# Context of tile 0 loaded ahead of the positions; VectorE's work of the first steps, a bank and the turned maxima of tile 3 ordered anew

## The chip, the core and the metric

The kernel runs on one core of one Trainium2 chip. A core has TensorE (PE, matrix products, which go to PSUM), VectorE (DVE), ScalarE (ACT), GpSimd (POOL), and SyncE (SP), which here only issues DMAs. Every engine works through its own instructions in order and waits on semaphores for the others. The metric is the device time of one execution in microseconds (us); lower is better.

## What is computed

One transformer block on 1024 tokens of 512 features, in fp32: cross attention with rotary positions and 32 heads that share 8 key and value heads, then a mixture of low-rank experts. In batches of 64 tokens each query sees the 64 context rows of its own batch.

```python
def block(x, c, pos):
    h = layernorm(x)
    q, k, v = h @ Wq, c @ Wk, c @ Wv
    q, k = q*cos + rotate_half(q)*sin, k*cos + rotate_half(k)*sin
    p = softmax(q @ k.T / sqrt(16))          # 32 heads of 16, 8 of k and v
    x = x + (p @ v) @ Wo
    h = layernorm(x)
    scores = (h @ Wr.T) @ keys.T             # 64 experts, the best 16 of them
    gate = softmax over the best 16, 0 elsewhere
    z = (h @ A.T) * gate for each group of 8 columns
    return x + (z @ B.T) * 2
```

## The kernel before

The tokens are 8 tiles of 128. Large products are done with operands split into a high and a low part (hi, lo): ScalarE rounds the high part, VectorE or GpSimd subtracts to get the low part, and TensorE adds three products (hi by hi, hi by lo, lo by hi). Tile 0 and the keys and values of tile 1 are done raw, in full fp32, since their weights are not split yet.

The order of every engine is written out by hand in five stages: `first()`, `second()`, `step(i)` for i = 1 and 2, `late_step(i)` for i = 3 to 5, and `last()`. In step i the attention of tile i is finished, the scores of tile n = i + 1 are made, q, k and v of tile p = i + 2 are projected, and, from i = 2 on, the experts of tile f = i - 2 are done. Step 1 has no tile f; it does work that comes once instead. Engines meet through counting semaphores, and several PSUM banks (ps_t0, ps_t1, ps_w0, ps_w1, ps_s) have many users one after another.

What the change touches:
- The head. ScalarE's queue issues the positions (`pos_sb`, L609) and the context of tile 0 (`cT_in`, L610). SyncE's queue issues x of tile 0, then the weights. VectorE copies the positions (L1174) ahead of aggregating the statistics of tile 0; from these GpSimd makes 1/std (L412) and VectorE xh (L1191), the normalised x, which TensorE turns (L1359).
- `attend(t, meanwhile)` on VectorE: a transpose of the sums of values (o_s, L1052), reciprocals (L1057), a product (o_t, L1061), a transpose back (o_n, L1067). `meanwhile` is work between the first transpose and the reciprocals. `q_low(t)` is the low part of the turned q (qT_lo, L1009).
- `top(t, b)` takes maxima of the scores, `m_parts(t)` splits them (m_split, L1044 and L1046), TensorE turns them (`turn_m`, L1458), and ScalarE copies them out: `m_out`, one copy of mT (L695) up to tile 2, two large copies into q_stack (L691) from tile 3 on. Then come the turned scores (L1483; L1470 for the stacked tiles 3 to 6), ScalarE's exponentials (L702) and the values (L1500).
- From tile 4 on, q is projected from the raw x (`DIRECT = 4`), and its mean is taken out with the negated column sums of Wq. `wq_sum` adds them, `sum_columns` (L1401) spreads them with TensorE into the bank `SUMS`, and `sums_out` copies them (L645). `statistics1(t)` (L943 to L952) and GpSimd's `deviation1(t)` (L412, then cs_q) give mean and 1/std of tile t.
- `residual(t)` adds x (L1075) and makes the mean x_mean (L1080), which ScalarE's centred x (x_c, L717) needs; `x2_low` is L1095. In step 2 `route(0)` is the choice of experts, whose last instruction makes gate (L1127). `split_lo` on GpSimd makes the low parts of weights, b_lo among them (L403).
- `up_high(f)` on TensorE is the high part of the experts' last product, eight matmuls in chunks k = 0 to 3.

Two rules of the code on banks matter: `qT_bank(3)` is ps_t0, and so is `kT_bank(3)`; `x2T_bank(0)` and `x2T_bank(1)` are ps_t1.

Of the kernel before, what the change touches and what calls it, by code (L numbers as in the profile page):

```python
# [21 lines left out]
FIRST = 3  # L22
STACKED = (3, 4, 5, 6)
QUADS = (4, 5, 6, 7)
DIRECT = 4
# [32 lines left out]
def build(nc, x, xT, cT, pos, wq, wqT, wkv, wo, aT, router, bT, out):  # L58
    ctx = ExitStack()
    with ctx:  # L60
# [130 lines left out]
        def x2_of(t):  # L191
            return (x2[:, 0, :], x2[:, 1, :], wq_sb[:, 0, :])[t % 3]

        SUMS = ps_t1[:]

        def wqT_of(k):
            return (xT_raw[:].rearrange("p k q -> p (k q)"), res[:], z_sb, zg)[k]
# [20 lines left out]
        def qT_bank(t):  # L218
            return ps_t1 if t > LATE else ps_t0
# [180 lines left out]
        def _(pool):  # L400
            def split_lo(lo, raw, hi, high, low, k):
                pool.wait_ge(high, k + 1)
                pool.tensor_tensor(lo[:, k, :], raw[:, k, :], hi[:, k, :].bitcast(F32),  # L403
                                   ALU.subtract).then_inc(low, 1)

            def deviation1(t):
                pool.wait_ge(stat1, 3 * t + 3)
                if t >= 1:
                    pool.wait_ge(xh_ok, min(t, DIRECT))
                if t > DIRECT:  # L410
                    pool.wait_ge(cs_q_ok, t - DIRECT)
                pool.tensor_tensor(rstd1[:], ve1[:], neg_half[:], ALU.pow).then_inc(rstd1_ok, 1)  # L412
                if t >= DIRECT:
                    pool.wait_ge(rstd1_ok, t + 1)
                    pool.wait_ge(q_rot, 2 * t)
                    pool.tensor_scalar(cs_q[:], cs[:, t, :], rstd1[:], None, ALU.mult).then_inc(cs_q_ok, 1)
                elif t >= 1:
                    pool.wait_ge(rstd1_ok, t + 1)
                    pool.tensor_scalar(shift1[:], mv1[:, 0:1], rstd1[:], -1.0, ALU.mult, ALU.mult)\
                        .then_inc(shift1_ok, 1)  # L420
# [125 lines left out]

            def step(i):
                f, n, p = i - 2, i + 1, i + 2
                if p >= DIRECT:
                    deviation1(p)  # L550
                if f >= 0:
                    gated(f)
                else:
                    split_lo(b_lo, b_sb, b_hi, b_h, b_l, 0)
                deviation2(i - 1)
                o_low(i)
                k_blocks(p, 0)
                k_blocks(p, 1)
                if f < 0:
                    x_low(p + 1)  # L560
                rotated_q(p)
                if f >= 0:
                    x_low(p + 1)
                c_low(p + 1)
                if f < 0:
                    for k in range(1, DK):
                        split_lo(b_lo, b_sb, b_hi, b_h, b_l, k)
# [38 lines left out]

        @block.scalar
        def _(act):
            act.dma_start(pos_sb[:], pos).then_inc(ld_pos, 16)  # L609
            act.dma_start(cT_in[:, 0], cT[0]).then_inc(ld_c[0], 16)  # L610

            def split_hi(hi, raw, high, k):
                act.activation(hi[:, k, :], raw[:, k, :], ACT.Copy).then_inc(high, 1)
# [321 lines left out]
        def _(dve):  # L935
# [45 lines left out]
            def k_low(t):  # L981
                dve.wait_ge(kT_hi_ok, t + 1)
                if t >= 1:
                    dve.wait_ge(k_bd_ok, 2 * t)
                dve.tensor_tensor(kT_lo[:], kT_bank(t), kT_hi[:].bitcast(F32), ALU.subtract)\
                   .then_inc(kT_lo_ok, 1)
# [250 lines left out]

            def second():
                rotate_k(2)
                q_low(1)  # L1240
                attend(0)
                top(1, 0)
                top(1, 1)
                m_parts(1)
                k_low(2)
                rotate_q(2)
                x_low(3)
                residual(0)
                statistics2(0)

            def step(i):
                f, g, n, p = i - 2, i - 1, i + 1, i + 2
                if p >= DIRECT:
                    statistics1(p)
                if f >= 0:
                    route(f)
                    x2_low(g)
                attend(i, lambda: q_low(n))
                rotate_k(p)
                top(n, 0)  # L1260
                if f >= 0:
                    rotate_q(p)
                top(n, 1)
                k_low(p)
                if f < 0:
                    m_parts(n)
                    x2_low(g)
                    rotate_q(p)
                else:
                    m_parts(n)  # L1270
                    z_low(f)
                residual(i)
                statistics2(i)
                if f >= 0:
                    result(f)
# [60 lines left out]
        def _(pe):  # L1336
# [77 lines left out]
            def turn_q(t):  # L1414
                pe.wait_ge(q_r_ok, t + 1)
                pe.wait_ge(kT_lo_ok, t + 1)
                turn(qT_bank(t), q_r, REP).then_inc(qT_ps, 1)

            def quad_scores(t):
# [101 lines left out]

            def turn_x2(t):
                pe.wait_ge(x2_c_ok, t + 1)
                if t == 1:
                    pe.wait_ge(sums_ok, 1)
                turn(x2T_bank(t), x2_c, DK).then_inc(x2T_ps, 1)

            def down_high(t, half, chunks=range(DK)):
# [99 lines left out]
            def step(i):  # L1628
                f, g, n, p = i - 2, i - 1, i + 1, i + 2
                turned_scores(i)  # L1630
                if f >= 0:
                    pe.wait_ge(x2_ok, i)
                    project_down(f, 0)
                    if f >= 1:
                        pe.wait_ge(res_ok, f)
                    else:
                        pe.wait_ge(q_rot, 2 * p)
                    project_q(p, [0, 1])
                    pe.wait_ge(z_ok, 2 * f + 1)
                    project_down(f, 1)  # L1640
                    turn_x2(g)
                else:
                    pe.wait_ge(q_rot, 2 * p)
                    project_q(p, [0, 1, 2])
                values(i)
                turn_q(n)
                if f < 0:
                    turn_x2(g)
                if f >= 0:
                    pe.wait_ge(z_ok, 2 * f + 2)  # L1650
                else:
                    pe.wait_ge(x2_ok, i)
                project_kv(p)
                if f >= 0:
                    project_q(p, [2])
                scores(n, 0)
                scores(n, 1)
                if f >= 0:
                    pe.wait_ge(x2T_lo_ok, i)
                    turn_zg(f)  # L1660
                    turn_k(p)
                project_q(p, [3]).then_inc(q_ps, 1)
                if f < 0:
                    turn_k(p)
                pe.wait_ge(v_st_ok, p + 1)
                project_out(i)
                if f >= 0:
                    pe.wait_ge(q_rot, 2 * p + 2)
                    up_high(f)
                turn_m(n)  # L1670
                if f >= 0:
                    up_low(f)
                    turn_q(p)
                else:
                    pe.wait_ge(x2T_lo_ok, i)
                    sum_columns()

            def late_step(i):
# [152 lines left out]
```

## Time and profile before

| | before |
|---|---|
| median of 3 runs | 167.12 us (166.97 to 168.05) |
| the profiled execution | 167.25 us, span 165.5 us |
| PE busy | 159.5 us, 96% of the span |
| DVE busy | 135.7 us, 82% |
| ACT busy | 95.3 us, 58% |
| POOL busy | 89.5 us, 54% |
| chain that ended last, by engine | PE 78%, DVE 12%, issue 4%, DMA 3%, ACT 2% |
| TensorE's granted clock | 1.00 of full speed |

The span runs from the first to the last instruction of the profiled execution. The chain is followed back from the last instruction, at each step to what released it. TensorE is busy nearly throughout; it stands still in the first 6 us and at a few waits.

### The profile page before, as it was taken

The numbers are of one execution on the slowest core, as the hardware profiler recorded it, in microseconds if no ns is written. First come the engines' busy times: TensorE is split into PE (matmuls) and PEld (weight loads), VectorE is DVE, ScalarE is ACT, GpSimd is POOL, SyncE is SP. The second block draws the span as 40 slices with busy tenths as digits, with TensorE's granted clock in tenths as the row PEclk, the third lists the DMA queues.
The fourth block names the chain that finished last, engine by engine and source line by source line (L and its number), as shares of the span: only waits on it lengthen the run. The fifth ranks groups of instructions, "written<-read, shape, count | busy, mean of one in ns | idle before, by whom it ended". The sixth has DMA issues, their size and how long they took to land.

```text
span 165.5 us, 4197 instructions
## 1 busy us (share of the span) xinstructions
PE 159.5 (96%) x1437; PEld 128.8 (78%) x1437; DVE 135.7 (82%) x394; ACT 95.3 (58%) x215; POOL 89.5 (54%) x115
## 2 busy tenths in 40 slices
PE   7799999999999999999999999999999999999993
PEld 2556786777878887879888888979789886789883
DVE  1969886995998899799888998799886999868562
ACT  3588999899657443942579147842479065414210
POOL 6479999999889843724942099015360304220300
DMA  4999962303315234426452453114410000000013
GB/s 142 380 411 388 408 200 67 133 4 122 99 32 160 50 92 99 119 54 181 101 125 54 114 151 87 47 46 145 101 52 31 4 0 29 36 2 4 0 63 127
DMA packets 12116, 18.45 MB, mean 111 GB/s; under 512 B 2496, under 2 KB 5056, under 8 KB 11840
## 3 DMA queue, kind: packets, MB, share of 16 engines
q1 hardware_dynamic: 11808, 17.93, 34.9%
q10 hardware_dynamic: 288, 0.27, 0.5%
q8 instruction: 11, 0.18, 0.5%
q14 instruction: 9, 0.07, 0.1%
HBM read 11.11 MB, written 2.10 MB: 80 GB/s over the span
## 4 chain that ended last, share of the span: by engine, by line
PE 78%; DVE 12%; issue 4%; DMA 3%; ACT 2%; ACTq 0%; DVEq 0%
PE ps_w L1346 12%; PE ps_w L1347 11%; PE ps_w L1351 10%; PE ps_t L1359 6%; PE ps_s L1430 4%; PE ps_w L1339 3%; PE ps_w L1341 3%; PE ps_w L1340 3%; DVE ps_s L1034 3%; DMA cT_in<-cT 3%; PE ps_t L1500 3%; PE ps_s L1470 2%; PE ps_w L1563 2%; PE ps_w L1569 2%; PE ps_t L1351 2%
## 5 line engine op out<-in xcount | busy, mean ns | idle before, releaser
L481 POOL TENSOR_TENSOR late<-late,gate 128x512 f32<-128x512 f32 x7 | 7.6, 1081 | 32.6 <-DVE gate L1127 17.6
L702 ACT ACTIVATE eT<-ps_s 128x512 f32<-128x512 f32 x32 | 17.0, 602 | 1.8 <-PE ps_s L1489 1.0
L466 POOL TENSOR_TENSOR oT_lo<-o_n,oT_hi 128x512 fp32r<-128x512 f32 x8 | 10.4, 1295 | 9.0 <-ACT oT_hi L710 9.0
L1346 PE MATMUL ps_w<-am_hi,x2T_hi 128*128 128x288 f32 x44 | 12.7, 311 | 0.0
L1347 PE MATMUL ps_w<-am_lo,x2T_hi 128*128 128x288 f32 x44 | 12.0, 296 | 0.0
L1346 PE MATMUL ps_w<-b_hi,zT_hi 128*128 128x512 f32 (+1 forms) x28 | 11.0, 399 | 0.0
L412 POOL TENSOR_TENSOR rstd<-ve,neg_half 128x1 f32<-128x1 f32 x8 | 4.4, 554 | 12.2 <-DVE ve L952 10.8
L1024 DVE TENSOR_REDUCE ps_s<-ps_s 128x8 f32<-128x512 f32 x16 | 10.6, 688 | 0.3 <-PE ps_s L1430 0.2
L1034 DVE TENSOR_REDUCE ps_s<-ps_s 128x8 f32<-128x512 f32 x16 | 10.4, 691 | 0.5 <-PE ps_s L1449 0.3
L1339 PE MATMUL ps_w<-wq_hi,xT_hi 128*128 128x512 f32 x26 | 10.7, 413 | 0.0
L754 ACT ACTIVATE zT_hi<-ps_t 128x512 fp32r<-128x512 f32 x7 | 4.2, 598 | 11.2 <-PE ps_t L1359 11.2
L1347 PE MATMUL ps_w<-b_lo,zT_hi 128*128 128x512 f32 (+1 forms) x28 | 10.5, 379 | 0.0
L1341 PE MATMUL ps_w<-wq_hi,xT_lo 128*128 128x512 f32 x26 | 10.3, 395 | 0.0
L1340 PE MATMUL ps_w<-wq_lo,xT_hi 128*128 128x512 f32 x26 | 10.3, 394 | 0.0
L691 ACT ACTIVATE q_stack<-ps_s 32x1024 fp32r<-32x1024 f32 x8 | 7.7, 1010 | 4.2 <-PE ps_s L1458 4.2
L740 ACT ACTIVATE late<-ps_w 128x288 f32<-128x288 f32 x5 | 2.1, 412 | 13.1 <-PE ps_w L1351 13.0
L1346 PEld LDWEIGHTS ps_w<-am_hi,x2T_hi 128*128 128x128 f32 x44 | 8.3, 189 | 1.1 <-ACT late L736 0.4
L437 POOL TENSOR_TENSOR q_r<-q_a,q_b 128x512 f32<-128x512 f32 x7 | 9.1, 1295 | 0.0
L663 ACT ACTIVATE v_bd<-v_st 64x64 f32<-64x64 f32 x32 | 8.1, 252 | 0.6
L1347 PEld LDWEIGHTS ps_w<-am_lo,x2T_hi 128*128 128x128 f32 x44 | 8.3, 189 | 0.0
L426 POOL TENSOR_TENSOR cT_lo<-cT_in,cT_hi 128x512 fp32r<-128x512 f32 x6 | 7.8, 1294 | 0.0
L1009 DVE TENSOR_TENSOR qT_lo<-ps_t,qT_hi 128x512 fp32r<-128x512 f32 x8 | 5.4, 680 | 2.8 <-ACT qT_hi L679 2.8
(283 smaller groups left out, 554.0 us busy)
## 6 DMA issues: line engine op xcount, KB each, us to landing
x_sb<-x SPq DMA_DIRECT2D x8, 256.0 KB, 7.0
q_stack<-qT_hi SPq DMA_DIRECT2D x32, 64.0 KB, 2.0
cT_in<-cT SPq DMA_DIRECT2D x7, 256.0 KB, 3.8
out<-res SPq DMA_DIRECT2D x7, 256.0 KB, 2.0
wq_sb<-wq SPq DMA_DIRECT2D x4, 256.0 KB, 5.2
late<-wo SPq DMA_DIRECT2D x1, 1024.0 KB, 7.9
am_sb<-aT SPq DMA_DIRECT2D x1, 1024.0 KB, 9.3
b_sb<-bT SPq DMA_DIRECT2D x1, 1024.0 KB, 7.8
```

The source lines that it names most:

```text
L437: pool.tensor_tensor(q_r[:].rearrange("p (r k d) -> p k r d", r=REP, k=KVH), q_a[:].rearrange("p (k r d) -> p k r d", r=REP, k=KVH), q_b[: ...
L466: pool.tensor_tensor(oT_lo[:], o_n[:].rearrange("p (b r q) -> p r b q", b=2, r=REP), oT_hi[:].bitcast(F32), ALU.subtract).then_inc(oT_lo_o ...
L702: act.activation(eT[:, c].rearrange("p b n -> p (b n)"), ps_s[:, c, :], ACT.Exp)\
L1024: dve.tensor_reduce(neg_top[:, b, :, rp].rearrange("p (c h) -> p c h", h=2), ps_s[:, :, at:at + P].rearrange("p c (h k) -> p c h k", h=2), ...
L1034: dve.tensor_reduce(neg_top[:, b, HALF_H * half:HALF_H * (half + 1), :], ps_s[:, 2 * (1 - b) + half, :].rearrange("p (r h k) -> p h r k", ...
L1339: pe.matmul(dst, hi(k), w_hi[:, k, cols], start=(k == 0), stop=False)
L1340: pe.matmul(dst, hi(k), w_lo[:, k, cols], start=False, stop=False)
L1341: mm = pe.matmul(dst, lo(k), w_hi[:, k, cols], start=False, stop=(k == DK - 1))
L1346: pe.matmul(dst, hi(k), w_hi[:, k, cols], start=(k == 0), stop=False)
L1347: pe.matmul(dst, hi(k), w_lo[:, k, cols], start=False, stop=False)
L1351: mm = pe.matmul(dst, lo(k), w_hi[:, k, cols], start=False, stop=(k == DK - 1))
L1359: mm = pe.transpose(dst[:, P * k:P * (k + 1)], src[:, P * k:P * (k + 1)], ident[:])
```

## The change

It has five edits in the order of work, and one of a bank.

ScalarE issues the context of tile 0 ahead of the positions. The rows of ScalarE's queue at its start, before (-) and after (+), where pos_sb holds the positions and cT_in the context:

```order
-L609 DMA pos_sb<-pos 128x8
-L610 DMA cT_in<-cT 128x512
+L609 DMA cT_in<-cT 128x512
+L610 DMA pos_sb<-pos 128x8
 L766 ACT_TABLE_LOAD
```

The two loads change places; nothing else moves on ScalarE.

On VectorE, in `second()`, around `attend(0)`: L1009 is `q_low(1)`, L1052 the transpose of the values of tile 0, L1057 the reciprocals.

```order
-L1009 TENSOR_TENSOR qT_lo<-ps_t,qT_hi 128x4x2x64
 L1052 STREAM_TRANSPOSE o_s<-ps_s 128x1024
+L1009 TENSOR_TENSOR qT_lo<-ps_t,qT_hi 128x4x2x64
 L1057 RECIPROCAL ps_s<-o_s 128x16 x2
 L1061 TENSOR_TENSOR o_t<-o_s,ps_s 128x16x16 x2
```

`q_low(1)` has moved behind the transpose. The statistics of tile 4 (L943, L950, L952) have moved from the start of step 2 to the end of `second()`, and GpSimd's `deviation1(4)` with them, to the start of step 1.

On VectorE in step 1, behind the maxima of tile 2 (L1034): L985 is kT_lo of tile 3, L1044 and L1046 split the maxima, L1075 and L1080 are the residual of tile 1 and its mean, L1095 is x2T_lo of tile 0.

```order
 L1034 TENSOR_REDUCE ps_s<-ps_s 128x8 x4
-L985 TENSOR_TENSOR kT_lo<-ps_t,kT_hi 128x128
-L1044 CAST m_split<-ps_s 128x8x16
-L1046 TENSOR_TENSOR m_split<-ps_s,m_split 128x8x16
+L1044 CAST m_split<-ps_s 128x8x16
+L1046 TENSOR_TENSOR m_split<-ps_s,m_split 128x8x16
+L985 TENSOR_TENSOR kT_lo<-ps_t,kT_hi 128x128
+L1075 SCALAR_TENSOR_TENSOR late,x_sum<-ps_w,x_sb 128x512
+L1080 TENSOR_SCALAR x_mean<-x_sum 128x1
 L1095 TENSOR_TENSOR x2T_lo<-ps_t,x2T_hi 128x512
```

The maxima are split before kT_lo, and the residual and its mean stand ahead of x2T_lo and of rotating q, where they had been behind both.

The column sums go to the bank ps_t0. There they wait for kT_lo of tile 3, not for x2T_lo of tile 0, and it is the turning of q of tile 3 that waits until they are copied out, not the turning of x of tile 1.

On TensorE in step 2 the turned maxima of tile 3 come ahead of the last chunk of `up_high(0)`, 0.5 us of matmuls earlier in the order.

```diff
-        SUMS = ps_t1[:]
+        SUMS = ps_t0[:]
...
                 if t >= DIRECT:
                     pool.wait_ge(rstd1_ok, t + 1)
-                    pool.wait_ge(q_rot, 2 * t)
+                    if t > DIRECT:
+                        pool.wait_ge(q_rot, 2 * t)
...
             def second():
                 rotate_k(2)
-                q_low(1)
-                attend(0)
+                attend(0, lambda: q_low(1))
...
                 statistics2(0)
+                statistics1(4)
...
             def turn_q(t):
                 pe.wait_ge(q_r_ok, t + 1)
                 pe.wait_ge(kT_lo_ok, t + 1)
+                if t == FIRST:
+                    pe.wait_ge(sums_ok, 1)
                 turn(qT_bank(t), q_r, REP).then_inc(qT_ps, 1)
...
             def turn_x2(t):
                 pe.wait_ge(x2_c_ok, t + 1)
-                if t == 1:
-                    pe.wait_ge(sums_ok, 1)
...
                 if f >= 0:
                     pe.wait_ge(q_rot, 2 * p + 2)
-                    up_high(f)
+                    up_high(f, [0, 1, 2])
                 turn_m(n)
                 if f >= 0:
+                    up_high(f, [3])
                     up_low(f)
                     turn_q(p)
                 else:
-                    pe.wait_ge(x2T_lo_ok, i)
+                    pe.wait_ge(kT_lo_ok, p + 1)
                     sum_columns()
```

## Rows read from the trace of the kernel before

**Rows 1.** The chain that ended last: start us, us, what.

```profile
1.22 4.38 DMA cT_in<-cT
...
47.24 0.65 PE ps_t L1401 x4
```

**Rows 2.** Timeline, 4 to 7 us: start, us, engine line op out<-in xcount [idle<-releaser].

```profile
4.23 0.15 DVE L1174 CAST pos_f<-pos_sb 128x8 f32<-128x8 int32 x1
...
5.51 0.54 DVE L1191 TENSOR_SCALAR xh<-x_sb,mv,rstd 128x512 f32<-128x512 f32 x1
...
6.67 0.60 PE L1359 MATMUL ps_t<-ident,xh 128*128 128x128 f32 x4
```

**Rows 3.** DMAs issued before 2 us (last column us to landing), traffic 2.5 to 3.0.

```profile
x_sb<-x SPq DMA_DIRECT2D x1, 256.0 KB, 2.8
cT_in<-cT ACTq DMA_DIRECT2D x1, 256.0 KB, 4.4
pos_sb<-pos ACTq DMA_DIRECT2D x1, 4.0 KB, 3.0
...
DMA packets 173, 0.17 MB, mean 337 GB/s; under 512 B 92, under 2 KB 92, under 8 KB 173
```

**Rows 4.** Timeline, 25 to 29 us: values, transpose and reciprocals of tile 0.

```profile
25.67 1.09 PE L1500 MATMUL ps_s<-eT,v_bd 64*32 64x256 f32 x32
...
27.02 1.24 DVE L1052 STREAM_TRANSPOSE o_s<-ps_s 128x1024 f32<-128x1024 f32 x1
...
28.30 0.37 DVE L1057 RECIPROCAL ps_s<-o_s 128x16 f32<-128x16 f32 x2
```

**Rows 5.** Timeline, 37 to 41 us: the same of tile 1.

```profile
37.79 1.09 PE L1500 MATMUL ps_s<-eT,v_bd 64*32 64x256 f32 x32
...
38.99 1.25 DVE L1052 STREAM_TRANSPOSE o_s<-ps_s 128x1024 f32<-128x1024 f32 x1 [1.83 <-PE ps_s L1500]
...
40.75 0.36 DVE L1057 RECIPROCAL ps_s<-o_s 128x16 f32<-128x16 f32 x2
```

**Rows 6.** Timeline, 45 to 48 us, end of step 1.

```profile
45.79 0.28 DVE L985 TENSOR_TENSOR kT_lo<-ps_t,kT_hi 128x128 fp32r<-128x128 f32 x1
45.98 0.28 DVE L1044 CAST m_split<-ps_s 128x128 fp32r<-128x128 f32 x1
...
47.12 0.38 ACT L695 ACTIVATE mT<-ps_s 128x256 fp32r<-128x256 f32 x1 [0.77 <-PE ps_s L1458]
...
47.82 0.39 PE L1483 MATMUL ps_s<-qT_hi,k_bd_hi 32*128 32x256 f32 x4
```

**Rows 7.** Timeline, 49 to 55 us, start of step 2.

```profile
49.21 0.72 ACT L717 ACTIVATE x_c<-late,x_mean 128x512 f32<-128x512 f32 x1 [0.68 <-DVE x_mean L1080]
...
50.10 0.68 DVE L943 BATCH_NORM_STATS2 bn<-x_sb 128x6 f32<-128x512 f32 x1
...
51.27 0.24 ACT L733 ACTIVATE s_sb<-ps_w 128x64 f32<-128x64 f32 x1
...
52.29 0.19 PEld L1346 LDWEIGHTS ps_w<-am_hi,x2T_hi 128*128 128x128 f32 x1 [0.42 <-ACT late L736]
...
54.71 0.56 POOL L412 TENSOR_TENSOR rstd<-ve,neg_half 128x1 f32<-128x1 f32 x1
```

**Rows 8.** Timeline, 65 to 69 us: the maxima of tile 3.

```profile
65.14 0.29 DVE L1046 TENSOR_TENSOR m_split<-ps_s,m_split 128x128 fp32r<-128x128 f32 x1
...
65.83 0.38 PE L1458 MATMUL ps_s<-ident,m_split 128*128 128x128 f32 x2
...
66.25 1.93 ACT L691 ACTIVATE q_stack<-ps_s 32x1024 fp32r<-32x1024 f32 x2 [2.82 <-PE ps_s L1458]
...
68.23 0.86 PE L1470 MATMUL ps_s<-q_stack,k_stack 128*128 128x256 f32 x5 [0.16 <-ACT q_stack L691]
```

**Rows 9.** Timeline, 50 to 55 us, then line L1127 in all: ns min/median/max.

```profile
50.96 3.80 POOL L403 TENSOR_TENSOR b_lo<-b_sb,b_hi 128x512 fp32r<-128x512 f32 x3
...
54.09 0.72 DVE L1127 TENSOR_SCALAR gate<-e_top,g_scale 128x64 f32<-128x64 f32 x1
...
L1127 DVE TENSOR_SCALAR gate<-e_top,g_scale x8: 254/255/724, 54.1 to 157.2; 128x64 f32<-128x64 f32 x8
```

More of the change, by code:

```diff
@@ L548, in step @@
                 f, n, p = i - 2, i + 1, i + 2
-                if p >= DIRECT:
-                    deviation1(p)
                 if f >= 0:
@@ L553, in step @@
                 else:
+                    deviation1(p + 1)
                     split_lo(b_lo, b_sb, b_hi, b_h, b_l, 0)
@@ L608, in _ @@
         def _(act):
+            act.dma_start(cT_in[:, 0], cT[0]).then_inc(ld_c[0], 16)
             act.dma_start(pos_sb[:], pos).then_inc(ld_pos, 16)
-            act.dma_start(cT_in[:, 0], cT[0]).then_inc(ld_c[0], 16)
             def split_hi(hi, raw, high, k):
@@ L1249, in second @@
                 statistics2(0)
+                statistics1(4)
             def step(i):
                 f, g, n, p = i - 2, i - 1, i + 1, i + 2
-                if p >= DIRECT:
-                    statistics1(p)
                 if f >= 0:
@@ L1263, in step @@
                 top(n, 1)
-                k_low(p)
                 if f < 0:
                     m_parts(n)
+                    k_low(p)
+                    residual(i)
                     x2_low(g)
@@ L1269, in step @@
                 else:
+                    k_low(p)
                     m_parts(n)
                     z_low(f)
-                residual(i)
+                    residual(i)
                 statistics2(i)
```

## The prediction

> **What bounds the kernel now.** I read the chain that ended last first. From 48 us to 128 us it is nearly all TensorE, piece after piece, so a delay or a gain that reaches TensorE before 68 us is carried to the end as it is. What matters is where, before that, the chain is not TensorE's own work. There are five such places, and each edit of this change touches one of them.
> The head: the chain starts with the load of the context of tile 0 (1.22 us, 4.38 long), and TensorE's first raw product follows at once [rows 1]. The second link is the first turned tile of x: VectorE copies the positions at 4.23, aggregates the statistics behind that copy, and writes xh from 5.51 to 6.05; TensorE turns it at 6.67 [rows 2]. So xh has some 0.6 us to spare and the context has none.
> `second()`: the values of tile 0 (25.67), the transpose (27.02), the reciprocals (28.30) [rows 4]. The chain passes over VectorE here.
> Step 1: the chain is VectorE's from 38.99 until the column sums, which TensorE starts at 47.24 once `x2_low(0)` is done [rows 1, 6].
> Step 2, two places: a weight load that waits for ScalarE's copy of z [rows 7], and the two big ScalarE copies of the turned maxima of tile 3, for which TensorE stands until 68.23 [rows 8].
>
> **The change part by part.**
> *1. Context ahead of positions.* The ScalarE queue now issues the context at 0.78 instead of 1.22 and the positions behind it. Landing took 4.4 us for the context, 3.0 for the positions and 2.8 for x of tile 0, which SyncE issued at the same moment [rows 3]. The context's data now runs beside those of x. From 2.5 to 3.0 us all queues together moved 337 GB/s [rows 3]; the context's 262 KB at that rate take 0.78 us, by which x can land later if the two share evenly (0 if x goes first). The positions' small packets no longer share x's time, so I take 0.70 rather than 0.78. The positions come last either way, but the bytes ahead of them are the same, so their landing is about that of the later of the two and adds nothing to it. The copy of the positions then moves from 4.23 to about 4.93, and xh ends at 6.75 instead of 6.05 [rows 2]. The context is there by then, so TensorE's first raw products are out of the way, and the turning starts at about 6.83 against 6.67: **+0.16**. Bounds: below, x and the positions not delayed at all, the turning starts 0.4 earlier, by the 0.44 that the issue moves less what TensorE needs after xh; above, the positions land only after a context that still takes 4.4 us, at 5.2, so the copy is 0.97 late, xh ends at 7.02, and the turning starts at 7.10: +0.43.
> The Trainium skill (DMA: Bandwidth & Descriptors, section Queues, rings and completion order) has the descriptors of one queue consumed in ring order on each DMA engine, and the engine taking turns between queues. No row of before shows a small transfer behind a large one on the ScalarE queue. By that rule the upper bound is a real possibility and not a mishap; it is the second rival below.
> *2. `q_low(1)` after the transpose of tile 0.* Before, it ran in VectorE's idle time ahead of the transpose. In step 1 the same pair already stands in the new order, so I read its cost there: values at 37.79, transpose 1.20 later, `q_low` behind it, reciprocals 1.76 after the transpose's start [rows 5]. Put on tile 0: values at 25.67, transpose 26.87, reciprocals 28.63, against 28.30 [rows 4]. The transpose starts 0.15 earlier and the reciprocals come 0.33 later: **+0.33**. All that follows on VectorE (the context of tile 0, the maxima of tile 1) and through ScalarE the output projection is on the chain. Bounds: -0.15, if the subtraction were free, and +0.58, the whole 0.69 less what starts early.
> *3. Statistics of tile 4 ahead of step 1.* Three VectorE instructions, one of 0.68 [rows 7] and two small ones, about 1.0 us together, move to where VectorE sat idle 1.83 us before the transpose of tile 1 [rows 5]; part 2 moves both ends of that gap, so they fit: 0. If the cover were gone they would cost 1.0. In step 2 they stood ahead of routing, which waited for s_sb anyway: 0 as well. GpSimd's pair (the power, 0.56 [rows 7], and cs_q, less than that) moves ahead of the first b_lo, where its later `o_low(1)` had idle time that part 2 only widens.
> *4. Column sums in the other bank, maxima of tile 2 first.* With the new order, m_split's cast starts where kT_lo started, 45.79, 0.19 before its old place [rows 6]; with the 0.33 of part 2 it is 0.14 later than before, and TensorE, whose output projection also slid 0.33, finds it ready. The sums now wait for kT_lo, which follows the two instructions of m_split (0.29 for one [rows 8]) and ends about 46.9, before TensorE has turned the maxima; the wait for x2T_lo is gone. What is late next is ScalarE's mT: it started at 47.12, now at 47.45, ends 0.37 later, and the turned scores start at about 47.86 against 47.82 [rows 6]. So of the 0.33 that came in, 0.04 goes out: **-0.29**. Bounds: 0, and -0.41 should mT not slide. Queued behind the moved kT_lo are GpSimd's k_bd_lo, x_low(4), c_low(4) and b_lo; rotating q of tile 3 falls behind the residual, so that b_lo starts about 1.35 late, but none is needed by TensorE for another 1 us or more.
> *5. Residual of tile 1 earlier.* ScalarE's x_c waited 0.68 for x_mean at 49.21, and its exponentials and s_sb (51.27) stood behind it [rows 7]. x_mean is now done before 48. At 52.29 a weight load had waited 0.42 for ScalarE's late (z) [rows 7], so that one load of 0.19 was exposed: **-0.15**. Bounds 0 and -0.26.
> *6. Maxima of tile 3 turned before the last chunk of `up_high(0)`.* m_split is ready at 65.14 + 0.29 = 65.43; TensorE turned it at 65.83, ScalarE began to copy at 66.25, and TensorE stood for the second copy until 68.23 [rows 8]. Now the turning starts at about 65.47. TensorE's other work is the same, plus an exposed weight load. 65.83 - 65.47 is 0.36, less a little for that load: **-0.33**. Bounds 0 (something else holds the stacked scores) and -0.41.
> Sum: 0.16 + 0.33 - 0.29 - 0.15 - 0.33 = -0.28 us. Span 165.5 becomes 165.2, and that execution, 167.25 with 1.75 around the span, 166.97. The median of the runs is 0.13 below it: 167.12 - 0.28 = **166.84, I say 166.85 us**.
>
> **The rivals.**
> *Slower: the gate of tile 0 misses its turn (0.10).* VectorE's gate took 0.72 at 54.09 and ended where a b_lo of GpSimd ended; its median over all tiles is 0.255 [rows 9]. GpSimd ran three b_lo from 50.96 in 3.80 us, 1.27 each [rows 9]. These now start about 1.35 later and end at 53.6, 54.8 and 56.1. A gate that starts near its old 54.09 is let go at 54.8 and x2T_lo is not late. If it starts after 54.8 it is held until 56.1, which is some 0.85 more than x2T_lo can bear; all of VectorE's step 2 up to m_split follows. Sum +0.57: 167.7. It decides from some 0.7 of delay in routing. Against it: routing starts earlier if part 5 holds.
> The Trainium skill (SBUF — State Buffer, on the shared pair of ports) calls this an exclusive lock held for a whole instruction; the trace agrees, 0.72 against 0.255.
> *No change: positions behind the context (0.20).* The upper bound of part 1, +0.43 in place of +0.16: sum -0.01, 167.1. It is what the ring order of the skill would make at its worst. For it: the context took 4.4 us, against 2.8 for x. Against it: the context then had the first weights beside it.
> *Faster: the head gains (0.17).* x is not slowed, and the positions land in time: -0.4 in place of +0.16: sum -0.84, 166.3. For it: the transfers of the first 3 us don't fill the engines at once. Against it: the rate from 2.5 us on.
> *Part 6 does nothing (0.08).* The stacked scores would stand on their DMAs, not on ScalarE's copy: sum +0.05, 167.2. Against it: the row at 68.23 names ScalarE [rows 8].
>
> **How the numbers follow.** Forecast 0.45, the rivals 0.10, 0.20, 0.17 and 0.08. The forecast alone gives 166.6 to 167.1 (parts 2 and 4 each to 0.2). Rivals reach from 166.3 to 167.7; leaving out a tenth on each side, the range is 166.2 to 167.6. A measurement of this kernel can tell about 1% (1.7 us) from no change. None of the cases reaches it. Only several bounds together would (-1.6 if all parts went well, +1.0 if all went badly), so faster by over 1% has 0.05, slower 0.03, within 1% 0.92.
>
> **What would show it.** Part 1: the copy of the positions at 4.9 (5.2 and later is the second rival, 4.3 the third), the first turning at 6.8. Part 2: reciprocals of tile 0 some 1.76 after the transpose's start. Part 4: column sums directly behind the turned maxima, the turned scores within 0.1 of where they would be without part 2's loss. Part 5: no wait of ScalarE's x_c for x_mean. Part 6: TensorE's wait for q_stack, 0.4 now, gone. The slower rival: a gate that ends after 55. The forecast would be wrong as a whole if TensorE were not continuous from 68 to 128 us and the gains were given back there, in waits for the stacked tiles' DMAs.

## The result

| | before | after |
|---|---|---|
| median of 20 runs each | 167.51 us (166.75 to 168.05) | 168.31 us (167.49 to 169.05) |
| ratio | | 1.0051, 95% interval 1.0038 to 1.0064 |
| the profiled execution | 167.25 us, span 165.5 us | 167.49 us, span 165.8 us |
| DVE busy | 135.7 us | 136.6 us |
| ACT busy | 95.3 us | 95.6 us |
| TensorE's granted clock | 1.00 | 1.00 |

The change makes the kernel slower by 0.5%, 0.85 us. The forecast was 0.28 us faster, 166.85 us, and its range ended at 167.6. The difference is within 1%, to which the forecast gave 0.92, but it is a loss where a gain was forecast. The profiled execution of the kernel after is the fastest of its 20, so its span is only 0.3 us above that of before: the traces below show where the time moves, the medians how much.

The first and the fourth part of the page of the kernel after: busy time of the engines, and shares of the span in the chain that ended last.

```profile
PE 159.3 (96%) x1437; PEld 128.6 (78%) x1437; DVE 136.6 (82%) x394; ACT 95.6 (58%) x215; POOL 89.6 (54%) x115
...
PE 52%; POOL 21%; SPq 9%; issue 7%; DVE 6%; DMA 4%; ACT 0%; ACTq 0%; POOLq 0%; DVEq 0%
```

The work is the same, but the chain is not. Before, 78% of it was TensorE's and SyncE's queue was not in it at all. Now it runs over GpSimd and then over SPq, SyncE's issuing of DMAs. The chain itself, kernel after, 48 to 69 us (start us, us, what):

```profile
48.55 1.31 POOL xT_lo L433
49.87 0.33 SPq L293
...
50.25 0.66 SPq L328
50.95 0.60 SPq L328
...
54.78 1.76 SPq L328
56.58 0.60 SPq L328
...
59.20 0.56 SPq L340
...
65.50 0.59 SPq L340
66.13 1.98 DMA q_stack<-qT_lo
68.16 1.22 PE ps_s L1472 x8
```

L293 is `load_xT(5)`, which may overwrite xT_raw only when GpSimd has made xT_lo from it. Queued behind it on SyncE are the copies that stack keys (L328) and turned queries (L340) of tile 3: 24 DMAs, 0.64 us from one issue to the next. The last is issued at 66.13 (before: 65.06) and lands 1.98 us later, and TensorE's stacked scores stand on it. Of the 1.07 by which it is later, 0.38 is there at the first stacked copy (49.87 to 50.25); the rest is nearly all one issue, the row at 54.78, of 1.76 us, where the longest before took 1.05. That part is mostly the draw of this one execution: in the 20 traces of this case the longest issue at this place takes 0.92 to 1.76 us, and this trace has the longest. What the change does to the queue is the 0.38; that it costs time in the medians too is shown by the experiments below and not by this trace.

### The profile page after: what moved, and what is told of

Its sections match the earlier page's. It is cut to its first block, busy times and chain, and to the rows that moved or that the text cites. A ratio compares the mean times of both kernels' runs of the same rounds, so it can differ in the third digit from the quotient of the medians.

```text
span 165.8 us, 4196 instructions
## 1 busy us (share of the span) xinstructions
PE 159.3 (96%) x1437; PEld 128.6 (78%) x1437; DVE 136.6 (82%) x394; ACT 95.6 (58%) x215; POOL 89.6 (54%) x115
## 4 chain that ended last, share of the span: by engine, by line
PE 52%; POOL 21%; SPq 9%; issue 7%; DVE 6%; DMA 4%; ACT 0%; ACTq 0%; POOLq 0%; DVEq 0%
PE ps_w L1346 8%; PE ps_w L1347 7%; PE ps_w L1351 7%; SPq L328 5%; PE ps_t L1359 4%; SPq L340 4%; PE ps_s L1432 4%; POOL am_lo L403 3%; POOL wo_lo L403 3%; POOL wq_lo L403 3%; PE ps_t L1502 3%; PE ps_s L1472 2%; POOL k_bd_hi L458 2%; DMA pos_sb<-pos 2%; PE ps_t L1346 2%
## 5 line engine op out<-in xcount | busy, mean ns | idle before, releaser
L1034 DVE TENSOR_REDUCE ps_s<-ps_s 128x8 f32<-128x512 f32 x16 | 10.4, 692 | 0.5 <-PE ps_s L1451 0.3
L1351 PE MATMUL ps_w<-am_hi,x2T_lo 128*128 128x288 f32 x44 | 7.6, 295 | 0.0
```

What stands on the lines that cost most here:

```text
L1034: dve.tensor_reduce(neg_top[:, b, HALF_H * half:HALF_H * (half + 1), :], ps_s[:, 2 * (1 - b) + half, :].rearrange("p (r h k) -> p h r k", ...
L1351: mm = pe.matmul(dst, lo(k), w_hi[:, k, cols], start=False, stop=(k == DK - 1))
```

## Where the parts moved things

The head. Landing of the first DMAs after issue (last column us), then the timeline, kernel after (start, us, engine, line, what, [idle before <- releaser]).

```profile
cT_in<-cT ACTq DMA_DIRECT2D x1, 256.0 KB, 3.5
x_sb<-x SPq DMA_DIRECT2D x1, 256.0 KB, 3.3
pos_sb<-pos ACTq DMA_DIRECT2D x1, 4.0 KB, 3.9
```

```profile
4.14 0.69 DVE L1172 BATCH_NORM_STATS2 bn<-x_sb 128x6 f32<-128x512 f32 x1 [2.95 <-DMA x_sb<-x]
...
5.06 1.10 PE L1563 MATMUL ps_w<-wkv_sb,cT_in 128*128 128x256 f32 x4 [0.17 <-issue]
...
5.17 0.17 DVE L1174 CAST pos_f<-pos_sb 128x8 f32<-128x8 int32 x1 [0.34 <-DMA pos_sb<-pos]
...
6.41 0.54 DVE L1191 TENSOR_SCALAR xh<-x_sb,mv,rstd 128x512 f32<-128x512 f32 x1
...
7.01 0.44 PE L1359 MATMUL ps_t<-ident,xh 128*128 128x128 f32 x2 [0.85 <-DVE xh L1191]
```

The context lands at 4.3 instead of 5.6 (0.79 + 3.5 against 1.22 + 4.4 [rows 3]) and TensorE's raw product starts 0.67 earlier. x lands later too: VectorE starts its statistics at 4.14 instead of 3.62, so 0.52 is lost there. The positions land at 5.15 instead of 3.8, VectorE stands at their copy for 0.34, xh comes 0.90 later in all, and TensorE then stands 0.85 for it: the first turned tile starts at 7.01 instead of 6.67 [rows 2].
The Trainium skill (DMA: Bandwidth & Descriptors, section Queues, rings and completion order) has descriptors of one queue consumed in ring order on each DMA engine. The traces agree: behind 256 KB the 4 KB of positions took 3.9 us, ahead of them 3.0, and they landed 0.9 us after the context.

`second()`. The same view, 26 to 30 us.

```profile
26.08 1.09 PE L1502 MATMUL ps_s<-eT,v_bd 64*32 64x256 f32 x32
...
27.28 1.25 DVE L1052 STREAM_TRANSPOSE o_s<-ps_s 128x1024 f32<-128x1024 f32 x1 [2.11 <-PE ps_s L1502]
...
28.46 0.65 DVE L1009 TENSOR_TENSOR qT_lo<-ps_t,qT_hi 128x512 fp32r<-128x512 f32 x1
...
29.03 0.36 DVE L1057 RECIPROCAL ps_s<-o_s 128x16 f32<-128x16 f32 x2
```

From the values to the reciprocals 2.95 us, against 2.63 [rows 4]; from the transpose to them 1.75, where the forecast read 1.76 off tile 1 [rows 5].

End of step 1 and start of step 2.

```profile
47.19 0.28 DVE L985 TENSOR_TENSOR kT_lo<-ps_t,kT_hi 128x128 fp32r<-128x128 f32 x1
...
47.55 1.04 POOL L458 TENSOR_TENSOR k_bd_lo<-kT_lo,half_mask 128x512 fp32r<-128x512 f32 x1 [0.87 <-DVE kT_lo L985]
...
47.82 0.38 ACT L695 ACTIVATE mT<-ps_s 128x256 fp32r<-128x256 f32 x1 [0.73 <-PE ps_s L1460]
...
48.25 0.39 PE L1485 MATMUL ps_s<-qT_hi,k_bd_hi 32*128 32x256 f32 x4
```

```profile
48.33 0.15 DVE L1080 TENSOR_SCALAR x_mean<-x_sum 128x1 f32<-128x1 f32 x1
48.55 1.30 POOL L433 TENSOR_TENSOR xT_lo<-xT_raw,xT_hi 128x512 fp32r<-128x512 f32 x1
...
48.88 0.72 ACT L717 ACTIVATE x_c<-late,x_mean 128x512 f32<-128x512 f32 x1
```

The reciprocals came in 0.73 late (28.30 to 29.03); the turned scores are 0.43 late (47.82 to 48.25), the values' transpose of tile 2 only 0.12 (55.86 to 55.98), so parts 4 and 5 gave back 0.30 and 0.31. But kT_lo is 1.40 late (45.79 [rows 6] to 47.19), and with it GpSimd's k_bd_lo, and xT_lo of tile 4, which ends at 49.85.

The maxima of tile 3.

```profile
65.25 0.29 DVE L1046 TENSOR_TENSOR m_split<-ps_s,m_split 128x128 fp32r<-128x128 f32 x1
...
65.59 0.44 PE L1460 MATMUL ps_s<-ident,m_split 128*128 128x128 f32 x2
...
66.07 1.93 ACT L691 ACTIVATE q_stack<-ps_s 32x1024 fp32r<-32x1024 f32 x2 [2.54 <-PE ps_s L1460]
...
68.16 1.10 PE L1472 MATMUL ps_s<-q_stack,k_stack 128*128 128x256 f32 x7 [0.28 <-DMA q_stack<-qT_lo]
```

m_split is 0.11 late, the turning 0.24 early, ScalarE's first copy 0.18 early (66.25 [rows 8] to 66.07). All eight stacked scores then run in a row from 68.16 (the eighth starts past this view's end), behind a wait for a DMA. Before, three of them ran from 67.47 on, and five from 68.23 [rows 8]. They end at 69.38 against 69.09: the 0.18 won has become 0.29 lost, and tile 7's values still carry 0.25 (139.56 to 139.81).

## The experiments

All are compared with the kernel before, measured beside it on the same chip. A ratio of 0.001 is 0.17 us. The 1.0051 of the whole change was measured apart from them, and the difference of two such ratios is uncertain by 0.4 to 0.6 us where nothing else is said. Line numbers shift by a few between kernels.

**The change less one part: head.** The kernel after with the positions first again.

```diff
-            act.dma_start(cT_in[:, 0], cT[0]).then_inc(ld_c[0], 16)
             act.dma_start(pos_sb[:], pos).then_inc(ld_pos, 16)
+            act.dma_start(cT_in[:, 0], cT[0]).then_inc(ld_c[0], 16)
```

> The changed kernel with the positions again ahead of the context on ScalarE's queue. Theory A (two early losses, the head and q_low of tile 1, that reach the end through SyncE's queue: they make x_low(4) late, which holds the load of xT of tile 5 and behind it the 24 DMAs of the stacked tile 3): the positions' copy back at 4.2, everything up to step 1 about 0.4 earlier, and since SyncE is then less late, 0.3 to 0.6 of the 0.85 given back: ratio to before 1.001 to 1.003. Theory B (the head is the whole loss, q_low and SyncE's queue cost nothing): ratio 0.998 to 1.000. Theory C (the head costs 0.35 to 0.4 in the first stage, but TensorE has made it up by the end, and the loss is elsewhere): ratio stays 1.004 to 1.006.

Measured 0.9992 [0.9969, 1.0016]. In the changed kernel the head costs 0.99 us (1.0051 less 0.9992; 0.5 to 1.4 by the two intervals). The ratio lies in theory B's range, but B also says that q_low and SyncE's queue cost nothing, and the runs below speak against that.

**Less q_low.** The kernel after with `q_low(1)` ahead of `attend(0)` again.

```diff
-                attend(0, lambda: q_low(1))
+                q_low(1)
+                attend(0)
```

> The changed kernel with q_low of tile 1 again ahead of the transpose of tile 0. Theory A: the reciprocals of tile 0 come 0.33 sooner behind the same head, 0.2 to 0.4 of the time is given back: ratio to before 1.002 to 1.004. Theory B: no difference from the changed kernel, 1.005. Theory C: 1.004 to 1.006.

Measured 1.0007 [0.9983, 1.003]: in the changed kernel it costs 0.74 us (0.3 to 1.2), more than the 0.2 to 0.4 that theory A expected.

**Less both**, which leaves parts 3 to 6.

> The changed kernel with both early edits undone; what is left are the edits of step 1, of step 2 and of the bank. Theory A: the stacked scores of tile 3 start no later than before, and the turned maxima 0.3 to 0.5 sooner; but kT_lo still stands behind m_split, so x_low(4) and SyncE's queue are some 0.2 to 0.5 late and take back a part: ratio to before 0.997 to 1.000. The prediction's sum (those edits give 0.77) says 0.995 to 0.996. Theory C: the loss is still there, 1.002 or more.

Measured 0.9954 [0.9927, 0.9981]: -0.77 us, the very sum of the forecast's parts 4 to 6, and better than the kernel before.

**Each alone on the kernel before**: the head, q_low, the turned maxima of tile 3, and parts 3 to 5 (the last is the kernel of parts 3 to 6 with the edit of `up_high` undone).

> The kernel before with the two loads of ScalarE's queue changed about and nothing else. If the head is a loss of its own (undoing it in the changed kernel took the ratio from 1.0051 to 0.9992): ratio to before 1.003 to 1.006, the positions' copy at 5.1 to 5.3. If the head costs only through SyncE's queue, which in the changed kernel had no slack left while here its last DMA of the stacked q lands 0.4 ahead of its use: 1.000 to 1.002. The prediction's step 1 says 1.001.

> The kernel before with q_low of tile 1 moved behind the transpose of tile 0 and nothing else. Priced from the traces: +0.33 us, the reciprocals 1.75 after the transpose's start: ratio to before 1.001 to 1.003. The rival, that the loss is absorbed in a wait before step 2: 0.999 to 1.001.

> The kernel before with the turned maxima of tile 3 one chunk of up_high earlier and nothing else. The prediction's step 6: -0.33 us, 0.997 to 0.999, the stacked scores' wait for ScalarE's copy gone. The rival: the DMAs of the stacked q land at 67.0 to 67.6 in this kernel too and the gain is capped by them: 0.999 to 1.001.

> The kernel before with parts 3 to 5 alone (statistics of tile 4 earlier, bank of the column sums, maxima of tile 2 split first, residual of tile 1 earlier); head, q_low and turned maxima as before. Theory A, the prediction's parts 4 and 5 hold by themselves: -0.44 us, 0.9974. Theory B, from the runs so far (parts 3 to 6 together -0.77, the turned maxima alone -0.08): -0.69 us, 0.9959, because part 6 is worth next to nothing with SyncE's queue where it is. Theory C, the gain of step 1 is taken at the stacked tiles too, since x_low(4) stands behind the moved kT_lo: 0.999 to 1.000. In the trace A and B want the stacked scores of tile 3 earlier against the head than the 60.80 us of before (67.47 less 6.67); C wants them where they were.

Measured: head 1.0036 [1.0023, 1.0048], +0.60 us; q_low 1.0039 [1.0025, 1.0053], +0.65 where 0.33 was priced; turned maxima 0.9995 [0.9982, 1.0008], -0.08; parts 3 to 5 0.9983 [0.9961, 1.0004], -0.28. The first two alone and parts 3 to 6 add to +0.48, and the whole measured +0.85. These 0.4 us are within the noise of four ratios (0.6), so the sum alone doesn't show that the parts disturb each other; the next experiment does.

Parts 3 to 5 alone came out between theories A and C, and the interval holds both. Their trace shows a gain that is taken back. Against the head the last five stacked scores of tile 3 are 0.49 earlier than before (67.37 less 6.30 against 68.23 less 6.67), those of tile 4 only 0.10. The last stacked copy of tile 4 is a long issue there (82.62, 1.66 us), and the chain runs over GpSimd's xT_lo and SyncE's queue as in the changed kernel:

```profile
PE 41%; SPq 21%; POOL 19%; issue 7%; DMA 5%; DVE 5%; ACT 0%; POOLq 0%; DVEq 0%
```

**SyncE's queue relieved in the changed kernel.** The stacked keys no longer stand behind the load that waits for xT_lo:

```diff
             load_x(7)
-            load_xT(5)
             stack_k(3)
+            load_xT(5)
             stack_q(3)
```

> The changed kernel with SyncE issuing the 12 DMAs of the stacked k of tile 3 ahead of the load of xT of tile 5, so that they don't wait for x_low(4). Both early losses stay. Theory A: the DMAs of the stacked q end 0.5 to 1.0 sooner, the stacked scores of tile 3 wait for ScalarE's copy again (about 68.0 and not 68.16, and all later runs that are worse gain more): 0.3 to 0.8 us off, ratio to before 0.999 to 1.003. Theories B and C: no difference from the changed kernel, 1.004 to 1.006.

Measured 0.9987 [0.9964, 1.0009]: from 1.0051, 1.07 us come back (0.6 to 1.5), rather more than theory A's 0.3 to 0.8. SPq, 9% of the chain of after, is gone from that of this kernel (fourth part of its page):

```profile
PE 84%; DVE 9%; DMA 2%; issue 2%; ACT 1%; ACTq 0%; DVEq 0%
```

**The queue longer in the kernel before**: two extra loads of 4 KB ahead of `stack_k(3)`, into a tile that nothing reads.

```diff
             load_xT(5)
+            for n in range(2):
+                sp.dma_start(spare[:, n], pos).then_inc(extra[n], 16)
             stack_k(3)
```

> The kernel before, with two extra small loads (the positions, into a spare tile that nothing reads) on SyncE's queue between load_xT(5) and stack_k(3): about 2 x 0.6 = 1.2 us more for that queue, nothing more for any other engine. Theory A, the queue of stacked copies has at most 0.4 us to spare in the kernel before (last issue 65.06, landing about 2 later, ScalarE's copies done 68.18): +0.5 to +0.9 us, 1.003 to 1.005, the stacked scores of tile 3 stand on the DMA of q_stack and not on ScalarE's copy. Rival, the queue has slack and what made the changed kernel slower lies elsewhere: 1.000, stacked scores at 67.5 to 68.2 and released by ScalarE.

Measured 1.0073 [1.0049, 1.0096]: +1.22 us for some 1.2 us of queue, more than the 0.5 to 0.9 expected. Its timeline at tile 3:

```profile
65.85 1.93 ACT L697 ACTIVATE q_stack<-ps_s 32x1024 fp32r<-32x1024 f32 x2 [2.82 <-PE ps_s L1464]
65.93 0.59 SPq L342 DMA_DIRECT2D q_stack<-qT_lo  x1
...
68.01 1.22 PE L1476 MATMUL ps_s<-q_stack,k_stack 128*128 128x256 f32 x8 [0.70 <-DMA q_stack<-qT_lo]
```

No other engine got any work, and the stacked scores stand 0.70 on the DMA. So SyncE's queue has little slack in the kernel before. By the interval's low end (0.82) it is at most 0.4 us. By the one trace of before it would be some 0.8 at tile 3: there the last stacked copy lands at 67.05, eight scores take 1.22, and they ended at 69.09. That trace is a favourable one: its long issue of 1.05 us is among the shortest at this place (0.92 to 1.76 in the 20 traces).

**The same relief on the kernel before and on three of the singles** (the swap of `load_xT(5)` and `stack_k(3)` of above added to each).

> The kernel before with SyncE issuing stack_k(3) ahead of load_xT(5), nothing else. In its trace ScalarE's copy ended the stacked scores' wait (row at 68.23) and the queue's landing was within 0.4 us of it. Theory A, the queue binds only in what the change adds: 0.999 to 1.000 (-0.2 to 0 us). Theory B, the queue binds in many executions of the kernel before as well, as the 1.22 us of e11 for 1.2 us of queue suggest: 0.996 to 0.998 (-0.3 to -0.6 us).

> e10 with the two loads of the head swapped. Against e10 in the same call. Theory A, the head's cost is its own: the same +0.6 us as without relief. Theory B, half of it came from the queue: +0.3 us, the mean shift of the first turned tile over the traces (7.02 against 6.73).

> e10 with q_low(1) behind the transpose of tile 0. Against e10 in the same call. Theory A, the rest of q_low's 0.65 us is put on at the queue: +0.33 us, the reciprocals' delay in every trace. Theory B, it is paid elsewhere on the way (ScalarE or GpSimd): +0.65 us again.

> e10 with the maxima of tile 3 turned one chunk earlier. Against e10 in the same call. Theory A, the turned maxima are worth their predicted 0.33 us once the queue of tile 3 is out of the way: -0.3 us. Theory B, tile 4's queue takes it back, as in the trace of e6 (stacked scores of tile 4 at 86.93): 0 to -0.1 us.

Measured: before 1.0002 [0.998, 1.0024]; head 1.0025 [1.0007, 1.0044]; q_low 1.0028 [1.0, 1.0055]; turned maxima 1.0003 [0.9978, 1.0027]. The relief alone brings nothing that can be measured, where in the changed kernel it brought 1.07: the queue of before is near the edge, not over it. Against the relieved kernel the head costs 0.38 us and q_low 0.43, less than the 0.60 and 0.65 without relief, but with intervals of about half a microsecond these differences aren't settled. Nor does the swap free these kernels of the queue: in the head's trace the last stacked copy of tile 3 (issued at 66.24, 1.98 to landing) still holds the scores (68.26), and in q_low's that of tile 4 (84.48, 1.99; scores at 86.51). The turned maxima bring nothing here either.

**Why the turned maxima bring nothing.** The trace of the kernel with that edit alone has its stacked scores of tile 3 at 67.92 with the first turned tile at 7.09 (before 67.47 and 6.67), its values' transpose of tile 3 0.29 earlier against the head, and loses 0.6 at tile 4, where it stands 0.32 behind before. Its timeline there:

```profile
82.46 1.23 SPq L340 DMA_DIRECT2D q_stack<-qT_hi  x2
83.72 1.77 SPq L340 DMA_DIRECT2D q_stack<-qT_lo  x1
83.85 1.93 ACT L691 ACTIVATE q_stack<-ps_s 32x1024 fp32r<-32x1024 f32 x2 [0.46 <-PE ps_s L1458]
...
86.93 1.22 PE L1470 MATMUL ps_s<-q_stack,k_stack 128*128 128x256 f32 x8 [0.38 <-DMA q_stack<-qT_lo]
```

and the kernel before at the same place:

```profile
82.83 0.59 SPq L340 DMA_DIRECT2D q_stack<-qT_lo  x1
83.47 1.31 SPq L305 DMA_DIRECT2D cT_in<-cT  x1
83.73 1.93 ACT L691 ACTIVATE q_stack<-ps_s 32x1024 fp32r<-32x1024 f32 x2 [0.46 <-PE ps_s L1458]
...
86.19 1.19 PE L1470 MATMUL ps_s<-q_stack,k_stack 128*128 128x256 f32 x8
```

One issue in this stretch takes over 1 us rather than 0.59. In before it is the load behind the last stacked copy, and harmless; here it is that last copy itself, whose data land at 86.89. The two kernels' SyncE programs are the same. In the relieved kernel with this edit it is again the last copy (83.82, 1.68) and the scores start at 86.94. These are single traces; the medians (-0.08 and +0.03 us) agree with them.

**The head's copy later.** The loads swapped, and VectorE's copy of the positions moved behind the aggregate and the add of epsilon.

```diff
-                dve.wait_ge(ld_pos, 16)
-                dve.tensor_copy(pos_f[:], pos_sb[:]).then_inc(rope_step, 1)
                 dve.wait_ge(stat1, 1)
                 dve.bn_aggr(mv1[:], bn1[:]).then_inc(stat1, 1)
                 dve.wait_ge(stat1, 2)
                 dve.tensor_scalar_add(ve1[:], mv1[:, 1:2], EPS).then_inc(stat1, 1)
+                dve.wait_ge(ld_pos, 16)
+                dve.tensor_copy(pos_f[:], pos_sb[:]).then_inc(rope_step, 1)
```

> The kernel before with the two loads of the head swapped (as in e4_head_alone, 1.0036), and in addition VectorE's copy of the positions moved behind the aggregate of tile 0's statistics and the add of epsilon. Theory A, the loss of the swap is VectorE standing at that copy with the statistics ready behind it: most of the 0.6 us comes back, 0.998 to 1.001, the first turned tile of x starts at 6.2 to 6.6 and not at 7.0. Theory B, the loss is x landing later beside the context: the first turned tile stays at 6.9 or later, 1.003. Theory C, the swap costs at the sines and cosines, whose angles need the positions: turned tile early, but 1.002 or more.

Measured 1.0024 [1.0014, 1.0034], +0.40 us. Its timeline:

```profile
5.09 0.17 DVE L1178 CAST pos_f<-pos_sb 128x8 f32<-128x8 int32 x1
...
6.16 0.54 DVE L1191 TENSOR_SCALAR xh<-x_sb,mv,rstd 128x512 f32<-128x512 f32 x1
```

No theory in full: VectorE no longer stands at the copy, but x itself is late beside the context (its statistics start at 4.05, before at 3.62), and xh still starts 1.07 after that copy, since four angle operations stand ahead of it in VectorE's order. Of the loss of the swap alone (0.60) 0.2 us comes back, which is within the noise (0.3). That more would with xh ahead of the angles wasn't tried.

**Versions that might beat both.** Parts 3 to 6 with the queue relieved; the same once more; the same with the head of the last experiment; the same with the stores of tiles 0 and 1 behind the stacked q of tiles 4 and 5.

> The changed kernel with both early edits undone, and SyncE issuing the stacked k of tile 3 ahead of the load of xT of tile 5. If SyncE's queue still took something back with both undone (0.9954): 0.992 to 0.995. If it had slack again by then: 0.995 to 0.997, the same as without the move.

> The kernel of e9 once more, beside e17: 0.993 to 0.997, below the kernel before by 0.5 to 1.1 us.

> e9_best (parts 3 to 6 of the change, head and q_low as before, the stacked keys ahead of load_xT(5) on SyncE: 0.995) with the head of e12_head_copy_later. If the late copy of the positions frees the head (theory A of e12), it ends 0.1 to 0.5 us below e9_best: 0.992 to 0.995. If the head is bound by the landing of x and the context, or the sines come late: 0.995 to 0.999, no better than e9_best.

> e9 (parts 3 to 6, stacked keys of tile 3 ahead of load_xT(5)) with store(0) and store(1) moved behind the stacked q of tiles 4 and 5. Against e18 in the same call. Theory A, tile 4's queue holds the stacked scores: 0.2 to 0.5 us below e18. Theory B, it doesn't, or the later store holds the next result: no difference, or up to 0.3 us above. In the trace A wants the stacked scores of tile 4 less than 18.2 us behind those of tile 3 (e9: 66.50 and 84.87, 18.37).

Measured 0.995 [0.9931, 0.9969] and, once more, 0.9972 [0.9945, 1.0]; with the late copy 0.9962 [0.995, 0.9975], no better; with the later stores 0.9942 [0.9911, 0.9974], 166.27 us against 166.76 for the repeat, measured beside it. All but the repeat lie below the kernel before by their intervals, by some 0.5%; that the relief or the later stores add anything to parts 3 to 6 (0.9954) isn't shown. The mark that was set for tile 4's queue in the expectation, less than 18.2 us, wasn't met: its stacked scores came 18.36 us behind tile 3's (66.56 and 84.92), and without the later stores 18.37 and 18.50.

## Why the prediction was wrong, by its steps

*Part 1, the head (+0.16).* This part failed, and its second rival, positions behind the context, came true: the copy is at 5.17 ("5.2 and later is the second rival"), xh at 6.41 to 6.95 (that rival said 7.02). The step that failed: the forecast reasoned that the positions' landing "is about that of the later of the two and adds nothing to it": x had landed at 4.1 and the context at 4.3, the positions at 5.15. The term before it held better: the copy was to move by 0.70 with x, and x is 0.52 late. The rival's price, +0.43, lies within the interval of the head alone (0.39 to 0.80).

In 13 traces with the positions first, the first turned tile starts anywhere from 6.05 to 7.18 (mean 6.61, seven of them at 6.33 or earlier); in five with the context first (and the positions copied as in the changed kernel) always at 6.94 to 7.14 (mean 7.02), within 0.1 us of the end of xh, which is late every time. With the positions first, xh is ready at 5.89 to 6.24, and what decides is how long TensorE's first four raw products take. In the changed kernel with the positions first again, the context is in by 5.19 and xh by 6.05, and the turning starts at 7.03:

```profile
5.19 2.04 PE L1563 MATMUL ps_w<-wkv_sb,cT_in 128*128 128x256 f32 x4
...
7.03 0.68 PE L1359 MATMUL ps_t<-ident,xh 128*128 128x128 f32 x4
```

The same four took 1.10 in before. Five of the 13 traces are like this one (1.52 to 2.04, turned at 7.03 to 7.18), eight are not (1.10 to 1.22, turned at 6.05 to 6.67; the means are 7.10 and 6.31). From one product to the next it is 0.42 us in the slow ones and 0.21 in the fast, the factor between TensorE's two clock levels (1.2 and 2.4 GHz), while the profile has a granted clock of 1.00 in both; what decides it no run here shows. So the head costs an execution some 0.7 us or nothing. The mean shift of 0.41 us depends on how many of each kind were drawn, and the trace of before, one draw, would give 0.34.

*Part 2, q_low (+0.33).* Right at its place, to 0.01 us. In the trace of that edit alone the values' transposes of tiles 3 and 4 are 0.38 and 0.41 late against the head. But the median moved by 0.65. The changed kernel with it and without it can be compared tile by tile (times from the first turned tile): the reciprocals of tile 0 are +0.33, the transpose of tile 3's values +0.57 (66.51 against 65.94), stacked scores of tile 4 +0.77 (79.44 against 78.67), as the medians say (0.74). The loss grows at the two places where TensorE meets the stacked copies.

*Part 3 (0).* No time shows there. The gate, the first rival's place, took 0.72 at 54.74, as before at 54.09 [rows 9]. It ended at 55.46, with the second b_lo and past the 55 that the forecast had set as that rival's sign. Its cost did not occur: x2T_lo started behind it at 55.38, before at 55.26, where it had stood 0.44 for ScalarE after the gate, and the values of tile 2 are only 0.12 late.

```profile
52.87 3.79 POOL L403 TENSOR_TENSOR b_lo<-b_sb,b_hi 128x512 fp32r<-128x512 f32 x3
54.74 0.72 DVE L1127 TENSOR_SCALAR gate<-e_top,g_scale 128x64 f32<-128x64 f32 x1
```

*Part 4 (-0.29).* Right for TensorE, -0.30. The sentence that failed stands at its end: what is queued behind the moved kT_lo, "but none is needed by TensorE for another 1 us or more". The one that waits is SyncE: x_low(4) frees the buffer of `load_xT(5)`, and 24 stacked copies are queued behind that load, the last one near to binding. The forecast followed GpSimd's late instructions to TensorE and not to the queue that waits for them.

*Part 5 (-0.15).* The wait was right, and ScalarE's x_c waits for nothing now; the size was not, -0.31 in the traces. About 0.25 of it comes at 52.3, near the bound of 0.26, and 0.07 at 49.04, where a weight load had stood 0.21 for VectorE's `late` and the forecast had no term.

*Part 6 (-0.33).* The turning moved as forecast, -0.35 (from +0.11 to -0.24), and alone it is worth nothing that can be measured, -0.08 (-0.30 to +0.13). The forecast gave "the stacked scores would stand on their DMAs" 0.08, against it the row at 68.23 that names ScalarE [rows 8]. That row names what came last in tile 3, in one trace of a kernel in which nothing had moved. With this edit alone the stacked scores of tile 3 wait for nothing (67.92, the last copy issued at 65.53) and tile 3 gains 0.29 against the head; what the forecast had not looked at is tile 4, where SyncE's queue ends in the same stacked copies and takes it back. In the changed kernel, with SyncE late, tile 3 itself stands on the DMA.

Through q_stack the forecast's sum was nearly right in the traces, -0.18 against -0.28, but by luck: part 5 makes up for the head. What it missed is that from there TensorE isn't continuous but meets SyncE's queue at tiles 3 and 4. It had named just this as what would make it wrong as a whole. Parts 3 to 6 without the two that cost are -0.77 (-1.22 to -0.32), as summed, but that doesn't confirm the terms: parts 3 to 5 alone gave -0.28 and part 6 alone -0.08. The 0.4 between is within the noise (0.6).

Put together with what was measured: the head's own 0.41, q_low's own 0.33 and the -0.77 of parts 3 to 6 make -0.03 us, uncertain by half a microsecond. The changed kernel with SyncE relieved measures -0.22 (-0.60 to +0.15), which agrees; without relief it is +0.85. So some 0.9 us (0.4 to 1.4) appears beside the parts' own costs, most of it only with the parts together, and goes when `stack_k(3)` no longer waits for xT_lo.

What stays open is where in the run that 0.9 is lost: between the traces of the changed kernel with and without relief the scores of tile 3 differ by 0.54 against the head (60.61 and 61.15) and those of tile 4 by 0.41 (79.03 and 79.44), half of the 1.07 between the medians. The trace of the changed kernel is the fastest of its 20 executions (167.49, median 168.31), so it can't show what an ordinary one loses. And the 0.2 to 0.3 us by which the singles exceed their own costs lie within the intervals of the relieved runs.

## What to carry to other kernels

An engine that only issues DMAs has a timeline too: with 24 issues of 0.64 us in a row, SyncE is a 15 us chain, and one load with a wait ahead of it makes the whole chain late. When work is moved on any engine, follow who waits for its buffers, DMA queues included, to the last transfer behind them, and read its landing next to the wait that the profile names. What the profile names as a wait's releaser is the last of several in one place: look for the same pattern in the next tiles before counting the gain. And the head of one trace is one draw: with the same order of loads the first turned tile came at 6.05 to 7.18, while a small load behind a large one was late in every trace.

## What the hardware showed

One SyncE issue near 83 and one near 109 us in all 20 traces of this case, one near 73 in 19 (0.76 at most there in the kernel after) and one near 55 in 19 (0.92 in the other), take 1.0 to 1.8 us instead of about 0.6, and each time the queue named q8, instruction, moves a packet between a microsecond before that issue and its end. The DMA view of the kernel after, 54 to 56 us (queue, kind: packets, MB, share of 16 engines):

```profile
q1 hardware_dynamic: 230, 0.09, 19.2%
q8 instruction: 1, 0.02, 4.3%
```

It looks as if SyncE stands while its program is loaded; that is a coincidence in time, not an experiment. Which instruction is hit shifts by one or two between kernels with the same SyncE program, as at tile 4 above, where TensorE stood 0.38 us for it. It may be part of why one kernel's executions differ by 1 us and more.
